# Value bias in four pieces, zero rows cleared later and in parts, mask rows of two key chunks copied at once

## What is computed

```python
def _L0_xattn_ref(q, k, v, attention_mask, Wq, bq, Wk, bk, Wv, bv):
    qp = (q @ Wq.T + bq).reshape(b, t_q, h, d // h).transpose(0, 2, 1, 3)
    kp = (k @ Wk.T + bk).reshape(b, t_kv, h, d // h).transpose(0, 2, 1, 3)
    vp = (v @ Wv.T + bv).reshape(b, t_kv, h, d // h).transpose(0, 2, 1, 3)
    scores = jnp.einsum('bhqd,bhkd->bhqk', qp, kp) / jnp.sqrt(jnp.float32(d))
    scores = jnp.where((attention_mask == 1)[:, None, :, :], -jnp.inf, scores)
    out = jnp.einsum('bhqk,bhkd->bhqd', jax.nn.softmax(scores, axis=-1), vp)
...
x = x + _L0_xattn_ref(_layernorm(x), ctx_1024, ctx_1024, mask, ...)
x = x + _L0_attn_ref(_layernorm(x), ...)
x = x + _L0_ffn_ref(_layernorm(x), ...)
```

## Time and profile before

| what | value |
|---|---|
| median of 3 runs | 2132.06 us (2130.95 to 2136.61) |
| the profiled execution's own time | 2116.67 us |
| its span, first to last instruction | 2114.6 us |
| PE busy | 1787.5 us, 85% |
| POOL busy | 1422.5 us, 67% |
| DVE busy | 1553.9 us, 73% |
| ACT busy | 1224.2 us, 58% |

### The profile page before, as it was taken

One profiled execution on the slowest core, in us unless ns is written; L12 is line 12 of the kernel. 1 busy time (PEld: TensorE's weight loads), 2 busy tenths in 40 slices (PEclk: granted clock), 3 DMA queues, 4 the chain that ended last, 5 costly groups with the idle time before them and its releaser, 6 DMA issues. The chain is left out here.

```text
span 2114.6 us, 63195 instructions
## 1 busy us (share of the span) xinstructions
PE 1787.5 (85%) x24267; PEld 1280.5 (61%) x24267; DVE 1553.9 (73%) x3043; ACT 1224.2 (58%) x1911; POOL 1422.5 (67%) x650
## 2 busy tenths in 40 slices
PE   4699888888888988998888988897858884799996
PEld 2366655666566665666566656664435564588885
DVE  5788887878887888888888887888577767344442
ACT  3377766767677676777676766764544431233331
POOL 3388977879889798898788987874345430244442
PEclk9899999999999999999999999997965555799998
DMA  6555556655576556655666556633634323477774
GB/s 174 125 100 114 112 112 115 140 108 110 111 147 119 107 112 118 145 113 112 115 142 117 114 111 133 128 63 61 216 114 138 111 83 139 140 231 228 220 234 122
DMA packets 175856, 277.70 MB, mean 131 GB/s; under 512 B 60164, under 2 KB 135748, under 8 KB 175571
## 3 DMA queue, kind: packets, MB, share of 16 engines
q1 hardware_dynamic: 165826, 260.64, 52.7%
q0 software_dynamic: 8832, 12.06, 2.9%
q10 hardware_dynamic: 946, 1.10, 0.2%
HBM read 163.02 MB, written 31.98 MB: 92 GB/s over the span
## 5 line engine op out<-in xcount | busy, mean ns | idle before, releaser
L420 POOL TENSOR_TENSOR p_sum<-p_sum,pT 128x1024 f32<-128x1024 f32 x288 | 699.1, 2428 | 62.7 <-ACT pT L671 46.7
L671 ACT ACTIVATE pT<-scored,lift 128x512 f32<-128x512 f32 (+1 forms) x832 | 545.9, 685 | 264.0 <-PE scored L789 252.3
L535 DVE CUSTOM_DVE_ANT_0 junk<-key_ring,mbias 128x898 bf16<-128x898 f32 (+1 forms) x512 | 510.6, 1023 | 100.6 <-issue 99.5
L789 PE MATMUL scored<-qst,kst 128*128 128x64 f16 x6656 | 319.6, 198 | 153.0 <-DVE qst L548 88.3
L789 PEld LDWEIGHTS scored<-qst,kst 128*128 128x128 f16 x6656 | 267.6, 102 | 255.3 <-issue 202.4
L401 POOL TENSOR_TENSOR cp<-cx,cp 128x768 f16<-128x768 f32 (+1 forms) x128 | 322.5, 2530 | 63.8 <-ACT cp L611 59.7
L555 DVE COPY kst<-mbias 64x6144 f16<-64x6144 f16 (+1 forms) x128 | 357.1, 2809 | 3.3 <-issue 0.3
L753 PE MATMUL key_ring<-wvp,cp 128*128 128x256 f16 (+1 forms) x2496 | 305.4, 273 | 3.3 <-DVE mx L535 2.9
L753 PEld LDWEIGHTS key_ring<-wvp,cp 128*128 128x128 f16 (+1 forms) x2496 | 233.0, 99 | 52.9 <-issue 17.7
L812 PE MATMUL o_acc<-pT,v 128*32 128x128 f32 x6656 | 240.7, 279 | 0.9 <-issue 0.5
L506 DVE SCALAR_TENSOR_TENSOR kl<-key_ring,bks,kh 128x384 f16<-128x384 f32 (+1 forms) x256 | 158.4, 633 | 90.2 <-ACT kh L645 86.8
(11 more groups left out here) (225 smaller groups left out, 2487.5 us busy)
## 6 DMA issues: line engine op xcount, KB each, us to landing
w1p<-wsp SPq DMA_DIRECT2D x23, 1408.0 KB, 8.5
cx<-in_ctxT SPq DMA_DIRECT2D x32, 833.0 KB, 12.5
msk<-in_mask SPq DMA_DIRECT2D x64, 400.2 KB, 8.4
cx<-in_ctxT SPq DMA_DIRECT2D x32, 768.0 KB, 8.6
wsp<-w_parts SPq DMA_DIRECT2D x24, 704.0 KB, 3.7
w2p<-wsp SPq DMA_DIRECT2D x23, 640.0 KB
kst<-kh SPq DMA_DIRECT2D x256, 52.1 KB, 2.3
kst<-kl SPq DMA_DIRECT2D x256, 52.1 KB, 2.3
```

The source lines that it names most:

```text
L420: pool.tensor_tensor(p_sum[:], p_sum[:], pT[:, u], ALU.add).then_inc(added, 1)
L535: dve.tensor_tensor_reduce(junk[:, n % 2, :, 0:MPAIR[half]], ring[:, at:at + 2, 0:MPAIR[half]], mbias[:, j, MS[2 * half]:MS[2 * half] + 2 ...
L671: act.activation(pT[0:n, u, HALF * half:HALF * half + HALF], scored[0:n, half, :], ACT.Exp, bias=lift[0:n, 0:1], scale=SSCALE).then_inc(ex ...
L789: mm = pe.matmul(scored[0:n, half, S * (h % PAIRS):S * (h % PAIRS) + S], kst[:, place, rows], qst[:, j, h, :], start=True, stop=True, skip ...
```

## The change

The bias is added by POOL in four pieces of four tiles: piece 0 at the head of period -1, piece 1 after CL0 and piece 2 after CL2 of that period, piece 3 after A8 of period 0. The memset of `kst` rows 32 to 63 leaves the head of POOL's list, is cut into four and follows the first `prepare_queries`; SP waits for it ahead of the first key stack. Moments and Newton chain of x chunks 1 to 3 are split: chunk 1 ahead of `keep_ql(1)`, moments of chunks 2 and 3 and their Newton chain inside period -1. XT1 and Q2 on PE, XC1 on ACT follow K1 and KH1 instead of K0 and KH0. ACT makes all four high context parts of batch 0 ahead of `keep_qh(0)`. `sel_q` is loaded by SP with the first constants instead of by ACT, and PE's wait for the other constants moves from ahead of period -1 to the first `turn_maxima`. In every period MA0 goes, and MA1 copies both chunks in one instruction of 16 x 768 elements; S0 waits for it.

```diff
+CLEARS = 4
...
-DVE_ORDER = steps("MA3 N KL0 ... MA2 X14 X15 SH MA0 MA1 SPR")
+DVE_ORDER = steps("MA3 N KL0 ... MA2 X14 X15 SH MA1 SPR")
...
-FIRST_PE = first(PE_ORDER, {("K", 0): [("XT", 1)], ("K", 1): [("Q", 2)], ...
+FIRST_PE = first(PE_ORDER, {("K", 1): [("XT", 1), ("Q", 2)], ...
-FIRST_ACT = first(ACT_ORDER, {("KH", 0): [("XC", 1)], ("KH", 1): [("QH", 2)], ...
+FIRST_ACT = first(ACT_ORDER, {("KH", 1): [("XC", 1), ("QH", 2)], ...
+FIRST_POOL = first(POOL_ORDER, {None: [("BV", 0)], ("CL", 0): [("BV", 1)], ("CL", 2): [("BV", 2)]})
+SECOND_POOL = first(POOL_ORDER, {("A", 8): [("BV", 3)]})
-FIRST_DVE = first(DVE_ORDER, {None: [("NX", 1)], ("KL", 1): [("QL", 2)], ("KL", 2): ...
+FIRST_DVE = first(DVE_ORDER, {None: [("NX", 1)], ("KL", 0): [("MO", 2)], ("KL", 1): [("QL", 2), ("MO", 3), ("NT", 2)], ("KL", 2): ...
...
-            init_done, N_INIT = sem("init_done"), 8
+            init_done, N_INIT = sem("init_done"), 7
...
                     def stack_keys(b, part):
+                        if isinstance(b, int) and b == 0:
+                            sp.wait_ge(rows_clear, CLEARS)
...
                     load_mask(0)
-                    sp.wait_ge(init_done, N_INIT)
                     turn_queries(0, 0)
...
+                    def add_bias(n):
+                        pool.wait_ge(consts_in, N_CONSTS)
+                        pool.wait_ge(s_xn, CT * n + CT)
+                        part = x_all[:, CT * n:CT * n + CT, :]
+                        pool.tensor_tensor(part, part, bv[:].unsqueeze(1).to_broadcast([P, CT, D]), ALU.add).then_inc(bv_added, 1)
...
-                        if isinstance(b, int) and b < 0:
-                            pool.wait_ge(s_xn, TILES)
-                            pool.tensor_tensor(x_all[:], x_all[:], bv[:].unsqueeze(1).to_broadcast([P, TILES, D]), ALU.add).then_inc(bv_added, 1)
-                    pool.memset(kst[32:64].rearrange("p h k -> p (h k)").bitcast(F32), 0.0).then_inc(init_done, 1)
-                    pool.wait_ge(init_done, N_INIT)
                     for n in range(KC):
                         low_context(0, 0, n)
-                    pool.wait_ge(consts_in, N_CONSTS)
+                    pool.wait_ge(first_in, N_FIRST)
                     pool.wait_ge(q_kept, DC)
                     prepare_queries(0, 0, 0)
+                    pool.wait_ge(qb_ready, 1)
+                    for n in range(CLEARS):
+                        part = slice(H // CLEARS * n, H // CLEARS * n + H // CLEARS)
+                        pool.memset(kst[32:64, part].rearrange("p h k -> p (h k)").bitcast(F32), 0.0).then_inc(rows_clear, 1)
+                    pool.wait_ge(rows_clear, CLEARS)
...
                     keep_ql(0)
+                    moments(1)
+                    dve.wait_ge(s_mv, 2 * CT)
+                    newton_rsqrt(dve, CT, CT, 1)
                     keep_ql(1)
-                    for n in range(1, NCH):
-                        moments(n)
-                    dve.wait_ge(s_mv, TILES)
-                    newton_rsqrt(dve, CT, TILES - CT, 1)
...
-                        dve.tensor_copy(kst[MASK_AT:P, :, chunk(c)],
-                                        mbias[MASK_AT:P, j, MS[c]:MS[c] + KWIDTH[c]].bitcast(F16).unsqueeze(1).to_broadcast([S, H, KWIDTH[c]])).then_inc(laid[c], 1)
+                        cols, at = (HALVES[0], 0) if c == 1 else (chunk(c), MS[c])
+                        w = cols.stop - cols.start
+                        dve.tensor_copy(kst[MASK_AT:P, :, cols],
+                                        mbias[MASK_AT:P, j, at:at + w].bitcast(F16).unsqueeze(1).to_broadcast([S, H, w])).then_inc(laid[c], 1)
...
+                            elif kind == "MO":
+                                moments(n)
+                            elif kind == "NT":
+                                dve.wait_ge(s_mv, TILES)
+                                newton_rsqrt(dve, n * CT, TILES - n * CT, 2)
...
-                    high_context(0, 0, 0)
-                    high_context(0, 0, 1)
+                    for n in range(KC):
+                        high_context(0, 0, n)
                     keep_qh(0)
-                    high_context(0, 0, 2)
                     keep_qh(1)
-                    high_context(0, 0, 3)
...
                         if step == 2 * GT * c:
-                            pe.wait_ge(laid[c], b + 1)
+                            pe.wait_ge(laid[max(c, 1)], b + 1)
...
                     def turn_maxima(b, j):
+                        if isinstance(b, int) and b == 0:
+                            pe.wait_ge(consts_in, N_CONSTS)
...
-                    pe.wait_ge(consts_in, N_CONSTS)
                     pe.wait_ge(init_done, N_INIT)
```

More of the change, by code:

```diff
@@ L96 @@
 POOL_ORDER = steps("QB A1 A2 A3 A4 A5 CL0 A6 A7 A8 A9 CL1 A10 CL2 CL3")
-DVE_ORDER = steps("MA3 N KL0 KL1 R X0 KL2 X1 KL3 KL4 X2 X3 KL5 X4 X5 KL6 X6 X7 KL7 X8 X9 X10 X11 X12 X13 MA2 X14 X15 SH MA0 MA1 SPR")
+DVE_ORDER = steps("MA3 N KL0 KL1 R X0 KL2 X1 KL3 KL4 X2 X3 KL5 X4 X5 KL6 X6 X7 KL7 X8 X9 X10 X11 X12 X13 MA2 X14 X15 SH MA1 SPR")
 SP_ORDER = steps("CX0 CX1 QS MK QR ST0 ST1")
@@ L110, in first @@
     return found
-FIRST_PE = first(PE_ORDER, {("K", 0): [("XT", 1)], ("K", 1): [("Q", 2)], ("M", 0): [("Q", 3)], ("K", 3): [("XT", 2)], ("M", 1): [("Q", 4)],
+FIRST_PE = first(PE_ORDER, {("K", 1): [("XT", 1), ("Q", 2)], ("M", 0): [("Q", 3)], ("K", 3): [("XT", 2)], ("M", 1): [("Q", 4)],
                             ("M", 2): [("Q", 5)], ("M", 3): [("XT", 3)], ("M", 4): [("Q", 6)], ("K", 6): [("Q", 7)]})
-FIRST_ACT = first(ACT_ORDER, {("KH", 0): [("XC", 1)], ("KH", 1): [("QH", 2)], ("KH", 2): [("QH", 3)], ("KH", 3): [("XC", 2)],
+FIRST_ACT = first(ACT_ORDER, {("KH", 1): [("XC", 1), ("QH", 2)], ("KH", 2): [("QH", 3)], ("KH", 3): [("XC", 2)],
                               ("KH", 4): [("QH", 4)], ("KH", 5): [("QH", 5), ("XC", 3), ("QH", 6)], ("KH", 6): [("QH", 7)]})
-FIRST_DVE = first(DVE_ORDER, {None: [("NX", 1)], ("KL", 1): [("QL", 2)], ("KL", 2): [("QL", 3), ("NX", 2)], ("KL", 4): [("QL", 4)],
+FIRST_POOL = first(POOL_ORDER, {None: [("BV", 0)], ("CL", 0): [("BV", 1)], ("CL", 2): [("BV", 2)]})
+SECOND_POOL = first(POOL_ORDER, {("A", 8): [("BV", 3)]})
+FIRST_DVE = first(DVE_ORDER, {None: [("NX", 1)], ("KL", 0): [("MO", 2)], ("KL", 1): [("QL", 2), ("MO", 3), ("NT", 2)], ("KL", 2): [("QL", 3), ("NX", 2)], ("KL", 4): [("QL", 4)],
                               ("X", 2): [("QL", 5), ("NX", 3)], ("X", 4): [("QL", 6)], ("KL", 6): [("QL", 7)]})
@@ L262, in program @@
             st_done, exp_done, added = sem("scoreT_done"), sem("exp_done"), sem("weights_added")
-            bv_added = sem("bv_added")
+            bv_added, rows_clear = sem("bv_added"), sem("stack_rows_clear")
             pv_done, sums_done = sem("pv_done"), sem("sums_done")
             rs_done, att_done, out_turned, res_done = (sem(n) for n in ("sums_inverted", "att_done", "out_turned", "residual_added"))
-            FIRST = [(ident[:], a["ident"]), (wq[:], a["xWqT"]), (bq[:], a["xbq"])]
+            FIRST = [(ident[:], a["ident"]), (wq[:], a["xWqT"]), (bq[:], a["xbq"]), (sel_q[:], a["sel_q"])]
             WEIGHTS = [(wk[:], a["xWkT"]), (wv[:], a["xWvT"]), (bk[:], a["xbk"])]
-            CONSTS = [(sel_q[:], a["sel_q"]), (minus[:], a["minus"]), (kst[0:1], a["shift"]), (qst[1 + 3 * DH:P], a["delta"]),
+            CONSTS = [(minus[:], a["minus"]), (kst[0:1], a["shift"]), (qst[1 + 3 * DH:P], a["delta"]),
                       (bv[:], a["xbv"].partition_broadcast(P))]
@@ L422, in period @@
                     def period(b, i, j, do_a, do_b):
-                        for kind, n in POOL_ORDER:
+                        for kind, n in (FIRST_POOL, SECOND_POOL)[b + 1] if isinstance(b, int) and b < 1 else POOL_ORDER:
                             if kind == "A" and do_a:
@@ L427, in period @@
                                 low_context(b + 2, j, n)
+                            elif kind == "BV":
+                                add_bias(n)
                             elif kind == "QB" and has_later(b):
                                 prepare_queries(b + 2, i + 1, j)
[L430 to L435 removed]
                     for n in range(KC):
                         low_context(0, 0, n)
[L439 removed]
+                    pool.wait_ge(first_in, N_FIRST)
                     pool.wait_ge(q_kept, DC)
                     prepare_queries(0, 0, 0)
+                    pool.wait_ge(qb_ready, 1)
[3 more added lines that the diff above has]
+                    pool.wait_ge(rows_clear, CLEARS)
                     periods(pool, period)
@@ L589, in _ @@
                     dve.wait_ge(mv3[0], TILES - CT)
-                    newton_rsqrt(dve, 0, TILES - CT, 2)
+                    newton_rsqrt(dve, 0, TILES - CT, 3)
                     normalize(B - 1)
@@ L1083, in _ @@
                     def _(dve):
-                        newtons = [3]
+                        newtons = [4]
                         def newton(at, w):
```

## The result

| | before | after |
|---|---|---|
| median of 8 runs | 2129.73 us (2101.07 to 2136.61) | 2145.49 us (2134.79 to 2149.43) |
| the profiled execution's own time | 2116.67 us | 2149.43 us |
| its span, mean granted TensorE clock | 2114.6 us, 0.895 | 2147.3 us, 0.875 |

The changed kernel takes 1.011 times the time of before, 95% interval 1.006 to 1.016: 15.8 us slower by the medians, and 23 (13 to 34) by this ratio, which is taken over the fast executions alone. Eight runs of each don't tell which is nearer the truth. The forecast was 2142, 10 us above the median it had. The two profiled executions are 32.8 us apart, twice the difference of the medians: that of before was a quick one, 13.1 us under its median, that of after 3.9 above.

The account below looks back on a forecast made before the run. No engine full; the first stage (to about 1460 us) is set by whichever wait ends last at its seams. Terms -5.7 (end of period -1), +2.6 (bias), +13 (merged copy) sum to +10 on median 2132.06: 2142 us, range 2119 to 2158.

Parts of the forecast that it names:

- The copy of two chunks: Every period's seam: merging saves 3.4 us fixed time but changes turns at the POOL/DVE port; net +13 us.
- seams B: Ten seams where POOL is one operation ahead and mask copies alone decide; merging starts K0 1.65 us earlier in each.
- A: Twenty seams where K0 hangs almost equally on CL3; with merging, MA3 precedes CL3 and K0 starts 1.6 us later.
- slower than forecast: Little of the seam A loss absorbed, B periods turn A: -3.5 + 3 + 30 - 5 = +24.5, 2157 us; chance 0.52 with forecast.
- the 5 us kept of the 16.5: Gain from earlier K0 in ten seams B: 16.5 us unabsorbed, 5 kept because most runs into the stacked-keys wait.
- 18 - 5: Copy term after absorption: 18 us kept of the 30 lost in seams A, less 5 gained in seams B.
- End of period -1: Bias piece 2 holds the port to 90.0, merged copy to 93.3, S0 about 94.7 instead of 100.42: -5.7 us.
- 2.0 us later for the rest of period -1: Lead-in: 4.2 us of moments and Newton chain ahead of first maxima, less 0.7 and 1.5; ends 0 and 4.2.
- Some 3 us that the earlier chain has to spare: Lead-in: high_contexts ahead of keep_qh wait for the second context half, covered by some 3 us of slack.
- Bias piece 3: After A8 in period 0, where POOL has no idle time: CL3 and K0 of period 1 come 2.6 us later (0 to 3).
- Faster: CL3 takes the port ahead of MA3, the 0.24 us margin being absent: -11 us, 2121; chance 0.24.
- No difference: Seams A and B cancel through waits elsewhere; lead-in's -3 remains, up to 8 us either side: 2129; chance 0.24.

Follow-up runs that it names:

- e2: The kernel before with only the mask copies of chunks 0 and 1 merged; 2146.58 us, ratio 1.007.
- e1: The changed kernel with the mask copies of chunks 0 and 1 apart again; 2131.56 us, ratio 0.998.
- e5: The kernel before with only DVE's division of the last result moved ahead of the third mask copy; 2133.61 us, ratio 1.000.
- e4: The changed kernel with sel_q loaded by ACT again and POOL's wait moved back with it; 2143.27 us, one run.
- e7: The changed kernel with the four clears at the head of POOL's list again; 2133.24 us, one run.
- e9: The changed kernel with both sel_q loaded by ACT and the clears at the head of POOL's list; 2146.08 us, one run.
- e3: The changed kernel with DVE's division of the last result moved ahead of the third mask copy (MA3); 2110.52 us, ratio 0.990.
- e6: The kernel before with merged copy, division ahead of the third copy, and bias in four pieces, three after CL0 of period -1; 2102.03 us, ratio 0.989.
- e8: The changed kernel with moments and Newton chain of x chunks 2 and 3 ahead of period -1 again; 2150.23 us, one run.

## Why the prediction was right, and where not

**The copy of two chunks: right in order and place; the size came out near, in part by luck.** Forecast +13 us. "Clean" says 1280.7 - 1268.1 = +12.6 (about 20 if the whole difference is taken from the ratio); e2, the copy alone, 15.8 us by the ratio 1.0074 (10 to 22), with a gain at K0(0) in it that period 0 gives back. The uncorrected traces say +29.6, which is the quick profiled run of before and not the change. One detail was wrong: seams B did not stay. Of the ten, one is left; the other nine turned into A, as the rival "slower than forecast" had it, so the 5 us kept of the 16.5 were not there. And the sum counted only when K0 starts. The windows above show that little of the loss is idle time of PE and most of it slower matmuls, for which the sum has no term. That 18 - 5 comes near the measured size is therefore luck as far as the parts go. How much waits elsewhere took up, a run doesn't tell apart. One of them is gone: ACT waited 13.0 us in 14 places for the stacked keys, in after 3.8 us once. "K0 to K0 up from 43.2 to 43.7": 43.28 to 44.30 by the two traces, up by 12.6 / 29 = 0.43 by the corrected ones.

The page that I weighed against this, Perfetto Trace Analysis of the Trainium skill, section "Optimizing Scalar/DVE Operations", would have had a gain of 3 us from grouping; e2 says a loss. The same section ties grouping to an engine that is saturated and adds that where it isn't but causes bubbles on others, breaking instructions up may finish work sooner. DVE is 73% busy here, and e1, with the copies apart, takes K0's waits from 28 to 1: the trace agrees with that second sentence.

**End of period -1: the step itself right, its place in time wrong.** From the end of piece 2 to S0 I had 4.7 us; it is 4.6 (95.5 to 100.1). But all of it lies 5.4 us later: "S0 at about 94.7" was 100.10, past my own bound of 98, and the term -5.7 came out as -0.3 (-1.9 against e5, which runs the instructions of before up to here; its S0 is at 102.04). It failed in the lead-in, with "2.0 us later for the rest of period -1". L555 ends 7.9 us later than in before and 6.3 later than in e5 (87.93); 6.6 are there at the first maxima against either:

- 4.3 are the last moments and the second Newton chain, from 47.59 to 51.87, straight ahead of the maxima. I had this price (4.2, with one set of moments and the chain) and took off "0.7" and "gaps in DVE's queue about 1.5". Nothing came off.
- 2.3 are the query block ahead of them (`keep_ql(2)`, 46.92 against 44.63). Two causes act, by one trace each: `sel_q` (e4), costed as "0.45 us of issue at an idle time", and the clears beside `normalize_x` (e7), costed as "not held", with 3 us as the other end. How they share the 2.3 stays open: e4 brings `keep_ql(2)` to 46.20, e7 to 45.77 and e9 to 45.44, while e1 and e3, with the lead-in of after, have it at 47.51 and 46.46. Of the gain at K0(0), 1.4 us in each of the three come only between the first maxima and the end of L555, and no run says why. The error in the first was to count the issue and not the landings: behind `sel_q` both context halves and x chunk 1 land 1.3 to 2.0 us later. In the second it was the argument from an instruction's duration to the port.
- "Some 3 us that the earlier chain has to spare" for the high contexts ahead of `keep_qh` weren't there either: PE waits 6.50 us at 23.93 for the query halves that ACT and DVE keep after them. No run took this part alone.

**Bias piece 3: right in kind, too small.** From K0(0) to K0(1) it is 46.05 instead of 41.45 us, +4.6; the forecast had 2.6 for the piece (0 to 3) and 1.6 for this seam as an A. But e1, with the piece and without the merged copy, takes 45.61 as well, +4.2: nearly all of it goes with the piece. POOL's last sum moves behind the end of L555 there, and both low contexts behind it, so that K0 waits 2.9 us. In e6, where POOL has no bias to add in period 0, it is 39.9.

**Sum.** -0.3 + 4.6 + 12.6, and -1.1 for the rest of the kernel, are the 15.8 measured (they must add up, since "clean" takes the correction); I had -5.7 + 2.6 + 13 = +10. The forecast was too low, by the lead-in above all and then by piece 3. If the ratio's 23 us is nearer the truth, the case "slower than forecast", at +24.5, was the better one. The -3.5 in its sum is not the -5.7 + 2.6 of the others.

**The rivals.** "Faster" hung on 0.24 us of margin and fell: MA3 had the port first in 28 seams. e3 makes that rival's order on purpose, and finds it worth more than I gave it (clean 1247.4, 21 us under before, where the rival had -8 for the seams). "No difference" fell by the interval.

## What to carry to other kernels

Where two engines exclude each other, merging two short instructions of one removes a turn of the other: ask who stands in the queue for the turn after, and put work that doesn't need the port there (here one swap of names turned +1.1% into -1.0%). What a load moved to the front costs is read at the landings behind it (here up to 2.0 us) and not at its issue (0.45). Gains ahead of a stage's first wait count only as far as the next resource is ready for them, and a single profiled run can sit 15 us off its own median: compare parts only after setting that right. A wait that moves from one item of an engine to the next adds little idle time; look at the busy time of the same instructions, and at the clock, before pricing it by its length.

## What I had not expected of the hardware

**Who gets the port.** It is settled within hundredths of a microsecond. Two mask copies in the trace of before and one in that of e5, each beside a POOL sum that is about to end:

```profile
1079.73 2.37 POOL L420 TENSOR_TENSOR p_sum<-p_sum,pT 128x1024 f32<-128x1024 f32 x1
...
1082.06 3.27 DVE L555 COPY kst<-mbias 64x6144 f16<-64x6144 f16 x1
1082.06 1.65 POOL L401 TENSOR_TENSOR cp<-cx,cp 128x768 f16<-128x768 f32 x1
```
```profile
780.01 2.38 POOL L420 TENSOR_TENSOR p_sum<-p_sum,pT 128x1024 f32<-128x1024 f32 x1
...
782.26 1.76 DVE L555 COPY kst<-mbias 64x6144 f16<-64x6144 f16 x1
782.34 3.18 POOL L401 TENSOR_TENSOR cp<-cx,cp 128x768 f16<-128x768 f32 x1
```
```profile
608.68 2.38 POOL L420 TENSOR_TENSOR p_sum<-p_sum,pT 128x1024 f32<-128x1024 f32 x1
...
610.98 1.76 DVE L555 COPY kst<-mbias 64x6144 f16<-64x6144 f16 x1
611.00 3.24 POOL L401 TENSOR_TENSOR cp<-cx,cp 128x768 f16<-128x768 f32 x1
```

In the first the two rows begin together, and DVE lost (3.27 us for a copy of 1.76). In the second DVE's begins 0.08 us earlier, in the third 0.02, and it won (POOL's 1.65 became 3.18 and 3.24). In the seam of after MA3's row begins some 0.2 us before CL3's, and it wins. The Trainium skill, SBUF — State Buffer, section "Who interferes with whom", says that whoever issues first gets the shared pair for the whole instruction; these rows agree. The turns of the prediction fit it too: POOL's next row begins only about where its last one ends, and a DVE row that has begun by then goes first.

**A short TENSOR_SCALAR can be held.** `normalize_x` runs 0.37 us alone, which the prediction took for a form that isn't held, yet beside POOL's memsets of about 2.8 us each (11.21 / 4) two of its four instructions lasted 2.75 and 2.93. In e8 even steps on 128x8 elements were held so (TENSOR_SCALAR at L195 and L196), while the TENSOR_TENSOR and SCALAR_TENSOR_TENSOR steps of the same chain, beside the last clear, ran in 0.17.

**The clock at the seam.** Windows in PE's wait ahead of K0 and in K0's six matmuls, at the seam between periods 1 and 2 of after (columns as above):

```profile
187.50:190.40 2.90, 0.00 (x0) 0.00 (x0) 2.84 (x2) 1.15 (x2) 2.90 (x2) 0.57 0.52 89
190.50:192.50 2.00, 2.00 (x7) 0.97 (x8) 0.33 (x1) 0.00 (x0) 0.45 (x1) 0.50 0.90 117
```

PE had stood still for 2.02 us ahead of S0 and for 2.95 ahead of K0. The granted clock fell during the second wait, and K0's six matmuls ran at 0.50, the lower of its two levels (1.2 GHz), in 2.10 us; in e6's row above they took 1.14. This isn't new with the change: in before S0's wait of 3.33 us stands just ahead, and K0's six matmuls take 2.11 in the earlier trace rows as well. It has become the rule: they take over 1.9 us in 21 of 31 seams of before, in 24 of e1, in 30 of after and in all 31 of e2. This is one way in which a seam costs PE busy time. What the lower clock alone costs no run separates from the waits that come with it.
